# One block instead of three: attention, router and expert mixture of a transformer layer on one NeuronCore

## What is computed

```python
h = _layernorm(x) * (1 + ca) + sa
x = x + ga * _L0_attn_ref(h, WQ, WK, WV, WO)      # softmax(QK^T/sqrt(8)) V, then @ WO.T
h = _layernorm(x) * (1 + cb) + sb
x = x + gb * _L0_ffn_ref(h, ...)
# inside _L0_ffn_ref:
shared = silu(x @ sg_w.T) * (x @ su_w.T) @ sd_w.T
scores = sigmoid(x @ gate_w.T) + gate_bias        # (tokens, 64)
# keep the 4 best of 8 groups of experts, then the 6 best experts, weights made to sum to 1 -> comb
h = silu(einsum('th,eih->eti', x, eg_w)) * einsum('th,eih->eti', x, eu_w)
routed = einsum('eti,ehi,te->th', h, ed_w, comb)
```

## Time and profile before

| | us |
|---|---|
| three runs | 1320.55, 1321.4, 1327.47 |
| median | 1321.4 |
| the profiled execution, whole | 1321.35 |
| its span, first to last instruction | 1319.3 |

### The profile page before, as it was taken

One profiled execution on the slowest core, in us unless ns is written; L12 is line 12 of the kernel. 1 busy time (PEld: TensorE's weight loads), 2 busy tenths in 40 slices (PEclk: granted clock), 3 DMA queues, 4 the chain that ended last, 5 costly groups with the idle time before them and its releaser, 6 DMA issues. The chain is left out here.

```text
span 1319.3 us, 14625 instructions
## 1 busy us (share of the span) xinstructions
PE 1141.1 (86%) x4104; PEld 482.5 (37%) x4104; DVE 802.6 (61%) x1447; ACT 584.8 (44%) x908; POOL 9.8 (1%) x28
## 2 busy tenths in 40 slices
PE   6689999999988389999999999758888798888698
PEld 3233333333333244444444444213333343333332
DVE  5767777666613935555555555467767766777355
ACT  4115555455543122222222222467666757666443
POOL 1000000000000000000000000000000000000000
PEclk9659999888887589999999999979988998899889
DMA  3701211100000045555555552100000000000001
GB/s 101 202 2 38 49 27 38 37 1 1 1 1 13 12 94 122 121 117 117 113 113 113 114 124 58 34 0 19 8 18 0 8 18 0 0 0 0 24 0 32
DMA packets 45292, 62.45 MB, mean 47 GB/s; under 512 B 16458, under 2 KB 38968, under 8 KB 39992
## 3 DMA queue, kind: packets, MB, share of 16 engines
q1 hardware_dynamic: 44420, 61.16, 20.1%
q10 hardware_dynamic: 832, 0.79, 0.2%
HBM read 55.87 MB, written 5.77 MB: 47 GB/s over the span
## 5 line engine op out<-in xcount | busy, mean ns | idle before, releaser
L685 DVE TENSOR_REDUCE part_max<-psum 128x1 f32<-128x512 f32 (+3 forms) x384 | 201.5, 553 | 88.9 <-PE psum L570 62.6
L657 ACT ACTIVATE pt<-psum 128x1024 f32<-128x1024 f32 (+1 forms) x192 | 152.5, 808 | 192.5 <-PE psum L588 153.2
L1077 DVE TENSOR_TENSOR moe_gu<-moe_silu,psum 128x512 f32<-128x512 f32 x132 | 90.7, 687 | 161.9 <-PE psum L1035 161.9
L1062 ACT ACTIVATE moe_silu<-psum 128x512 f32<-128x512 f32 x132 | 78.8, 597 | 235.5 <-PE psum L1026 235.5
L567 PE MATMUL psum<-ka,qa 72*128 (+4 forms) x384 | 134.2, 375 | 24.9 <-DVE part_max L685 15.7
L1026 PE MATMUL psum<-h,moe_wt 128*128 128x512 f32 x264 | 136.8, 600 | 0.6 <-ACT moe_wt L1055 0.6
L1035 PE MATMUL psum<-h,moe_wt 128*128 128x512 f32 x264 | 135.8, 596 | 0.0
L1017 PE MATMUL psum<-moe_hid,moe_wt 128*128 128x512 f32 x264 | 135.0, 593 | 0.7 <-DVE moe_hid L1086 0.7
L1299 PE MATMUL psum<-mix_c,wt_c 128*128 128x512 f32 x128 | 77.5, 725 | 41.4 <-ACT relu L1435 41.4
L585 PE MATMUL psum<-qa,ka 75*128 (+4 forms) x384 | 109.5, 348 | 4.1 <-DMA qa<-neg_t 2.5
L1086 DVE TENSOR_TENSOR moe_hid<-moe_gu,moe_comb 128x512 f32<-128x512 f32 x128 | 88.6, 692 | 16.7 <-DVE moe_gu L1077 8.0
(11 more groups left out here) (249 smaller groups left out, 1475.7 us busy)
## 6 DMA issues: line engine op xcount, KB each, us to landing
moe_comb<-comb_rows SPq DMA_DIRECT2D x64, 512.0 KB, 6.2
qa<-rows_q SPq DMA_DIRECT2D x24, 192.0 KB
ka<-rows_k SPq DMA_DIRECT2D x24, 192.0 KB
moe_raw<-in_L_ffn_eg_w SPq DMA_DIRECT2D x32, 64.0 KB, 5.7
moe_raw<-in_L_ffn_eu_w SPq DMA_DIRECT2D x32, 64.0 KB, 5.4
moe_raw<-in_L_ffn_ed_w SPq DMA_DIRECT2D x32, 64.0 KB, 5.1
rows_q<-part SPq DMA_DIRECT2D x4, 384.0 KB, 4.9
rows_k<-part SPq DMA_DIRECT2D x4, 384.0 KB, 4.9
```

The costliest lines, as they stand in the source:

```text
L657: act.activation(pt[:, u % 4, :, 0:n], score_bank[u % 2][:, :, 0:n], ACT.Exp, scale=SCALE)\
L685: dve.tensor_reduce(part_max[:, h, slot:slot + 1], max_bank[n % 2][:, 0:nk], AX_X, ALU.max)\
L1062: act.activation(sg[:, c % 2, :], g_bank[:, :], ACT.Silu).then_inc(silu_done, 1)
L1077: dve.tensor_tensor(gu[:, c % 2, :], sg[:, c % 2, :], u_bank[:, :], ALU.mult).then_inc(gu_done, 1)
```

## The change

The three stages become one, `stage_core`, with one block. It does the following.

- **Packed rows.** `normalise` writes to a small tile `o_spread`; four DMAs of 8 partitions x 512 (`pack`) then put each head's 8 rows at their place in `o` `[P, T]`. WO is no longer spread (`wo_sp`, its memset, copy and four transposes are gone), and `project` is one 512-column product per chunk. SP waits for `out_done` before each `pack`, and its group loop is written out instead of run as a loop.
- **Router inside the last group.** TensorE's and ScalarE's shares of the router for chunks 0 to 2 and the turning of the first four weight sets are called from `beside(u)` at fixed units of the last group. VectorE's share is written out in `last_group()`.
- **Expert slots.** The 16 (step, chunk) pairs of steps 0 to 3 (PRE = 4) run in the order `SLOTS`, which puts chunk 3 last, with the rest of the router between them (`prologue()` on each engine). Five weight tiles hold the first sets. Steps 4 to 32 run as before. ScalarE's tables for logarithm and exponential and for silu alternate in the prologue (four more `ACT_TABLE_LOAD`).
- **Factors.** The combination weights of the first four expert pairs are loaded chunk by chunk (`first_factors`, eight DMAs of 64 x 512 each) into the space of `qa` and `ka`.
- **Smaller routing.** The comparison and the multiplication that follow it are one operation (two operations fewer in a chain per chunk); some semaphores are merged.

```diff
-                    dve.tensor_tensor(G.o[:, g % 4, bass.ds((g // 4) * S + c * CH, CH)], acc[:, c, :], rden[:, c, :],
-                                      ALU.mult).then_inc(out_done, 1)
+                    if not isinstance(g, int) or g:
+                        dve.wait_ge(packed[c], PACKED * g)
+                    dve.tensor_tensor(o_s[:, c, :], acc[:, c, :], rden[:, c, :], ALU.mult).then_inc(out_done, 1)
...
-    for g in range(4):
-        mm = pe.matmul(G.bank[5 if c == 1 else 4][:, :], G.wo_t[:, g, :], G.o[:, g, chunk(c)], start=(g == 0), stop=(g == 3))
-    mm.then_inc(G.wo_psum, 1)
+                def project(c):
+                    pe.wait_ge(packed[c % 2], PACKED * 4 * (c // 2 + 1))
+                    pe.matmul(x_bank[c][:, :], G.wo_t[:, :], o[:, chunk(c)], start=True, stop=True).then_inc(wo_psum, 1)
...
+    STEPS, PRE = 33, 4
+    SLOTS = ([(0, 0), (0, 1), (0, 2)] + [(s, c) for s in range(1, PRE) for c in range(2)] + [(0, 3)]
+             + [(s, 2) for s in range(1, PRE)] + [(s, 3) for s in range(1, PRE)])
...
+                def beside(u):            # TensorE, last group
+                    if u == 0:
+                        pe.wait_ge(piece_max, NP * NG)
+                        project(0)
+                    if u == 2:
+                        centre(0)
+                    if u == 3:
+                        pe.wait_ge(den_log, 2 * LAST)
+                        turn_weights(0, 0)
+                    if u == 4:
+                        variances(0)
+                    if u == 7:
+                        logits(0)
...
+                    if u == 17:
+                        pe.wait_ge(ln.scaled, n0 + 2)
+                        project(2)
...
+                def pack(g, c):           # SyncE
+                    sp.wait_ge(out_done, 2 * g + c + 1)
+                    for h in range(HG):
+                        sp.dma_start(o[32 * (g % 4) + DK * h:32 * (g % 4) + DK * (h + 1), chunk(2 * (g // 4) + c)],
+                                     o_s[32 * h:32 * h + DK, c, :]).then_inc(packed[c], 16)
...
+                def prologue():           # VectorE
+                    route_scores(2)
+                    normalise(LAST, 1)
+                    slot(0)
+                    route_groups(2)
+                    slot(1)
+                    route_mask(2)
+                    slot(2)
+                    route_top(2)
+                    slot(3)
+                    add_attention(3)
+                    route_comb(2)
+                    slot(4)
+                    slot(5)
+                    modulated(3)
+                    slot(6)
+                    slot(7)
+                    route_scores(3)
+                    slot(8)
+                    route_groups(3)
+                    slot(9)
+                    route_mask(3)
+                    route_top(3)
+                    slot(10)
+                    route_comb(3)
+                    for n in range(11, 4 * PRE):
+                        slot(n)
```

865 lines of the change are left out of this document (500 added, 365 removed).

## The result

| | before | after |
|---|---|---|
| median, us | 1321.8 (1320.6 to 1327.5, 4 runs) | 1284.2 (1284.1 to 1285.0, 4 runs) |
| ratio to before, 95% interval | | 0.971 (0.968 to 0.974) |
| span of the profiled execution | 1319.3 | 1281.9 |

The changed kernel is 37.6 us faster; forecast were 38.3, and a time of 1283.

The account below looks back on a forecast made before the run. Bound: about 65 us of chained latencies between last group and expert slots. From 367.8, terms of 43.8, 60.7 and 308.3 end the slots at 780.6, not 818.9: 38.3 us off 1321.35 gives 1283 us, range 1266 to 1300.

Parts of the forecast that it names:

- The bound: Last output product to first gate product: about 65 us of chained latencies, beside which 352 us of expert slots could run.
- Term 1: Last group, with router work added and projection passes removed: grows from 34.4 to 43.8 us, ending at 411.6.
- Term 2: The 16 slots and the rest of the router: 60.7 us, bounds 48.6 to 71, slots ending at 472.3.
- Term 3: Expert steps 4 to 32: 29 steps of an unchanged 10.63 us, 308.3 us, ending at 780.6.
- Transfers and the groups ahead: Packing DMAs and factor loads hidden, chunk 3's pack with 2 us to spare; groups 1 to 6 lose 0.
- A: Joined stretch: overlap near perfect, TensorE's waits covered by other work in its queue; 1266 to 1272 us, chance 0.12.
- B: Joined stretch: chains bind more often, clock falls at each longer wait; 1292 to 1302 us, chance 0.22.
- C: TensorE runs the whole joined stretch at 1.2 GHz: slower, +62 us, 1345 us, chance 0.03.
- D: Slots: order worse than seen, a factor or pack late in several slots; 1302 to 1315 us, chance 0.06.

Follow-up runs that it names:

- before_again: The kernel before the change, unaltered, run once more for a second trace; 1325.5 us (one run).
- after_again: The changed kernel, unaltered, run once more beside the edited ones; median 1284.4 us.
- one_table: Changed kernel with the 16 silus of steps 0 to 3 computed as exponentials, without the table loads between them (outputs not the reference's); 1281.8 us.
- acc_early: Changed kernel with VectorE's last accumulator copy put ahead of the end of chunk 1's routing; 1284.2 us.
- turn_late: Changed kernel with chunk 3's turn of chosen, and its copy on ScalarE, one slot later, behind slot 11; 1281.9 us.
- slots_last: Changed kernel with all 16 slots behind the last turn of chosen, not mixed with the router's steps; router still beside the last group; 1301.3 us.
- pack2: Changed kernel with every packing DMA of groups 0 to 6 issued twice, VectorE waiting for both; 1283.8 us.
- both_waits: Changed kernel with the edits of turn_late and acc_early together; 1282.9 us.
- router_after: Changed kernel with chunks 0 to 2's router work and the four weight turns behind the last group, not beside it; slots still mixed; 1305.2 us.
- serial: Changed kernel with both overlaps taken back: router work behind the last group, all 16 slots behind the router; packing and joining kept; 1317.3 us.

## Why the prediction held, step by step

**The bound.** Right: the 65 us between the last output product and the first gate product were latency, and the work of the slots and of the router now shares them. What the forecast didn't count apart is how much of the saving is clock. By half of TensorE's busy time at clock 0.50, the low clock takes about 17.8 us of the stretch in before (14.2 in before_again) and 9.6 in after (7.9 in after_again): some 5 to 10 of the 38 us.

**Term 1, the last group, 43.8 us.** Measured 44.1 (365.69 to 409.78): nearly the right sum, with other parts, and so in part luck. The forecast's parts are 35.9 of work at full clock, 4.7 for the low clock (the 3.2 that the old group had, which are in its 39.1, and 1.5) and 3.1 of waits. Measured are about 35.0 of work, 4.4 for the clock and 4.8 idle. Logits 0 waited 1.31 (0.8 forecast), variance 2 1.27 (1.2), centring 1 0.61 (1.1). Not forecast were 0.94 at logits 1, whose chain I had taken to be covered, and 0.56 for the last exponentials. The clock's part also has another shape: the group's start is low for 5.3 us, not 6.4, and there is a second fall that I didn't have, from 381.2 to 384.7. It cost next to nothing, because VectorE's chain sets the pace there: from logits 0 to centring 1 it takes 6.29 us in after, and as much in after_again, where the fall comes later and TensorE waits 2.23 us instead of 0.61.

**Term 2, 16 slots and the router's rest, 60.7 us.** With the same bookkeeping (the slot's landmark at 778.94, less 29 steps of 10.63) it is 60.9. The forecast's parts are 48.6 of work, 7.1 of waits and 5.0 for the clock. TensorE is idle for 8.5 us (60.7 less 2.99 + 49.24 busy). It is busy for 5.7 us at clock 0.50 behind the first long wait and for 4.7 behind the second, of which half, 5.2, is the clock's: the price forecast. That leaves 47.2 for the work, 1.4 less than the 48.6. The reason is a landmark: 818.90 and 778.94 are the starts of the last but one down product, so that 46 slot products lie ahead of it, not the 48 of 16 slots, and two of them are 1.7 us. So waits 1.4 too low and work 1.4 too high cancel. The waits one by one: the last accumulator copy 2.09 (1.5 forecast); slot 11 4.60 (5.0), in the place and for the reason forecast; slots 6 and 8, where I had 0.7 for the table loads, 0.86 and 0.89, and one_table prices the loads at 3.1 to 3.2 us in all; the first silu 0 here and 0.59 in after_again (1.0). That two of the waits cost a fall of the clock besides was right at both places, and acc_early and turn_late take the falls away with the waits.

**Term 3.** Steps of 10.63 us, as forecast, in all 14 profiles.

**Transfers and the groups ahead.** Hidden, as forecast: the time to spare for the last pack, 2 us, comes out of slots_last's chain carried over to the changed kernel, and in acc_early, where the same reckoning leaves 0.2 us (issued at 416.11, 4.2 us to land, projection at 420.51), the projection doesn't wait either; pack2 shows the queue's room. Issuing one of these DMAs takes 0.62 to 0.73 us, not 0.5. The part ahead of the last group came out 2.1 us shorter, which can't be told from chance: in the kernels made from the changed one the last group starts anywhere from 363.6 to 371.4.

**The rivals.** A (1266 to 1272) did not occur; its condition, waits covered by other work, was missed at the two places named, and with both waits gone (both_waits) the stretch is 5.8 us shorter, not 12. B is what router_after, slots_last and serial show when an overlap is missing: waits after every step and a clock of 0.50 to 0.64 over 34 to 65 us. C had its condition, a bare chain of short products, in the same three kernels and not in the changed one, where PEclk is 0.90 in the last group and in the slots (0.71 over the 5 us between them). D is visible in turn_late (VectorE waits 3.17 us for factors, TensorE 1.28), where the slots have overtaken the factor loads, and nowhere in the changed kernel.

**What the forecast had wrong beyond sizes.** It had no term for the spread of the untouched stages, and that its centre was met in the whole time is luck to that extent. The saving of 37.6 us came out beside 38.3 with -2.1 ahead and +2.6 behind the stretch; with the first parts of serial (371.4) and the last part of router_after (503.5) the same stretch would give 5.7 + 3.4 = 9 us more, 1293, an estimate: still in the range, but no longer near the centre.

## What to carry to other kernels

Where one stage is a chain of short operations and the next a full queue, mix them in one program order; the gain is the chain's idle time and also its low clock, at which each product here took twice its time. In an in-order queue, put a step that waits for a long chain as late as its own users allow, and check what is next behind it: here the factor loads took back 1.5 of 5.0 us. Compare kernels by the stretch that the edit touches when the rest of the program varies by more than the edit is worth.
